# Layer-norm Newton steps on GpSimd, a routing store on ScalarE's queue, one bias tile, and the down products between gate and up

## The reference

```python
def ffn(x):                         # x: (4, 512, 256)
    w = golden_weights(x, Wr, temperature)      # 8 weights for each token
    gate = einsum('btd,edf->betf', x, Wg)       # 8 experts, F = 256
    up   = einsum('btd,edf->betf', x, Wu)
    e_out = einsum('betf,efd->betd', silu(gate) * up, Wd)
    return einsum('bte,betd->btd', w, e_out)

x = x + 0.5 * ffn(layernorm(x))
x = x + attention(layernorm(x))     # causal, 16 heads of 16, biases on q, k, v and the output
x = x + 0.5 * ffn(layernorm(x))
```

## Time and profile before

| | |
|---|---|
| three runs | 883.81, 884.58 (median), 886.05 us |
| the profiled execution, its time | 883.35 us |
| its span, first to last instruction | 881.6 us |
| TensorE busy | 792.5 us (90%) |
| VectorE busy | 508.9 us (58%) |
| GpSimd busy | 383.7 us (44%) |
| ScalarE busy | 344.4 us (39%) |
| mean granted TensorE clock | 0.973 |

### The profile page before, as it was taken

The page is one execution under the profiler, slowest core; times in us unless marked ns, Lnnn a source line. Parts: engine busy times, 40 slices in busy tenths (PEclk is TensorE's granted clock), DMA queues, the critical chain, the costliest instruction groups (busy, mean ns, idle before and its releaser), DMA issues.

```text
span 881.6 us, 13749 instructions
## 1 busy us (share of the span) xinstructions
PE 792.5 (90%) x4856; PEld 617.4 (70%) x4856; DVE 508.9 (58%) x1424; ACT 344.4 (39%) x656; POOL 383.7 (44%) x365
## 2 busy tenths in 40 slices
PE   3397897989988999979999897899999999999997
PEld 3286786857656676667767666677667677888886
DVE  5367677485666753586754466855446743475332
ACT  3134334424355343244533335444325344232321
POOL 3064564236432453242344334245344455446664
PEclk9889899999999999998999999999999999999999
DMA  4534433514412422221252213234222223222331
GB/s 155 168 108 144 120 109 96 140 53 108 106 58 77 121 74 86 60 72 55 84 151 73 73 55 90 73 109 108 94 76 73 74 73 96 72 72 80 125 108 49
DMA packets 60617, 81.93 MB, mean 93 GB/s; under 512 B 8066, under 2 KB 44162, under 8 KB 60548
## 3 DMA queue, kind: packets, MB, share of 16 engines
q1 hardware_dynamic: 58816, 80.90, 30.5%
q10 hardware_dynamic: 1732, 0.15, 0.1%
HBM read 68.17 MB, written 12.71 MB: 92 GB/s over the span
## 4 chain that ended last, share of the span: by engine, by line
PE 66%; DVE 21%; issue 3%; ACT 3%; DMA 3%; SPq 2%; POOL 1%; POOLq 0%; DVEq 0%; ACTq 0%
PE gu L408 10%; PE gu L410 10%; PE gu L409 10%; PE dn L427 5%; PE dn L428 5%; PE dn L429 5%; PE ra L517 4%; PE ra L490 4%; PE ra L505 3%; DVE junk L856 3%; PE ra L385 2%; DVE hid L821 2%; DVE hid L814 2%; PE ra L481 2%; SPq L992 1%
## 5 line engine op out<-in xcount | busy, mean ns | idle before, releaser
L912 POOL TENSOR_TENSOR hid<-hid,wb 128x512 f32<-128x512 f32 x128 | 167.7, 1311 | 299.0 <-DVE hid L821 267.0
L408 PE MATMUL gu<-xt_hi,wgu_hi 128*128 128x512 f32 x512 | 232.4, 454 | 16.6 <-DVE hid L814 16.6
L916 POOL TENSOR_TENSOR ht_lo<-hid,ht_hi 128x512 fp32r<-128x512 f32 x128 | 165.6, 1293 | 159.1 <-ACT ht_hi L619 159.0
L856 DVE CUSTOM_DVE_ANT_0 junk<-ra,mask 128x128 bf16<-128x128 f32 (+3 forms) x256 | 124.0, 488 | 161.0 <-PE ra L490 159.7
L410 PE MATMUL gu<-xt_lo,wgu_hi 128*128 128x512 f32 x512 | 206.1, 403 | 0.0
L409 PE MATMUL gu<-xt_hi,wgu_lo 128*128 128x512 f32 x512 | 204.9, 400 | 0.0
L427 PE MATMUL dn<-wd,ht_hi 128*128 128x256 f32 x512 | 164.8, 322 | 1.3 <-POOL ht_lo L916 1.3
L664 ACT ACTIVATE probs<-ra 128x512 f32<-128x512 f32 x160 | 95.4, 597 | 171.6 <-PE ra L505 170.9
L814 DVE SCALAR_TENSOR_TENSOR hid<-hid,gu 128x512 f32<-128x512 f32 x128 | 87.6, 684 | 122.4 <-ACT hid L612 121.9
L619 ACT ACTIVATE ht_hi<-hid 128x512 fp32r<-128x512 f32 x128 | 80.4, 628 | 187.9 <-POOL hid L912 166.9
L428 PE MATMUL dn<-wd,ht_hi 128*128 128x256 f32 x512 | 145.7, 285 | 0.0
(11 more groups left out here) (126 smaller groups left out, 859.2 us busy)
## 6 DMA issues: line engine op xcount, KB each, us to landing
wd<-wd_parts SPq DMA_DIRECT2D x56, 512.0 KB, 3.5
wb<-wts_rows SPq DMA_DIRECT2D x64, 256.0 KB, 3.9
qk_parts<-parts SPq DMA_DIRECT2D x32, 192.0 KB, 2.1
q_st<-qk_parts SPq DMA_DIRECT2D x96, 64.0 KB, 3.3
k_st<-qk_parts SPq DMA_DIRECT2D x96, 64.0 KB, 2.5
wd_parts<-wd SPq DMA_DIRECT2D x8, 512.0 KB, 5.1
x_res<-in_x SPq DMA_DIRECT2D x4, 512.0 KB, 6.5
stage<-in_Wg SPq DMA_DIRECT2D x8, 256.0 KB, 3.9
```

The source lines that it names most:

```text
L408: mm(b_, w_hi, xt_hi[q % 2][:, c, :], start=c == 0, stop=False)
L856: nc.vector.tensor_tensor_reduce(out=junk[:, USE[it] % NA, 0:w], in0=o[:, 0:w], in1=mask[:, T - w:T], scale=1.0, scalar=-3.0e38, op0=ALU.a ...
L912: nc.gpsimd.tensor_tensor(tb, tb, wb[m % NWB][:, :], ALU.mult).then_inc(hw_done, 1)
L916: nc.gpsimd.tensor_tensor(ht_lo[n % NHT][:, :], hid[n % NHID][:, :], f32(ht_hi[n % NHT][:, :]), ALU.subtract).then_inc(lo_done, 1)
```

## The change

1. **Newton.** Variance and seed stay on VectorE (now `var`), the three Newton steps and the shift go to GpSimd (`newton`, in two halves of 8 and 6 instructions, each waiting for the one before). [...] The first-layer blocks q = 1, 2, 3 are done together, on tiles of 12 instead of 4 columns, during chunks 3.6 to 5.4. There are then 10 sets instead of 12.
2. **Routing store.** For block 0 alone, the store of the weights and the first two loads back are issued by ScalarE right after its copy; ScalarE waits for the store to land before it issues the loads.
3. **Bias.** Since the weights of a token's attention sum to one, v's bias times Wo plus the output bias is one row for all tokens. It is computed once (6 matmuls, item `bias`) and added to the residual by GpSimd (`xb`, 8 additions of 128x512). The 32 matmuls of line 478 go, and so do the small set-up steps for `rows` and `ones`. The load of the output bias is now 128 KB.
4. **Order.** The down products of chunk n - 2 stand between gate and up of chunk n. The times of h, hi and lo move back by a third of a chunk.
5. **Small ones.** The memset of two rows of `k_st` (line 897) becomes a short memset and two small copies by ScalarE's queue. The first weight split (`sg`, 0) moves ahead of the first normalisation. Routing is cut into 8 pieces instead of 5, with the same instructions. The last addition and the output store of a block go in two halves, the first as soon as the first two token tiles are done.

```diff
@@ schedule()
+        put(n + 0.67, ("u", n, 0))
+        put(n + 0.83, ("u", n, 1))
+        put(n + 0.84, ("h", n))
-        put(n + 0.34, ("u", n, 0))
-        put(n + 0.50, ("u", n, 1))
-        put(n + 0.51, ("h", n))
         for i in range(QT):
-            put(n + LAG + 0.66 + 0.08 * i, ("d", n, i))
-        put(n + 0.85, ("hi", n))
-        put(n + 1.35, ("lo", n))
+            put(n + LAG + 0.34 + 0.08 * i, ("d", n, i))
+        put(n + 1.15, ("hi", n))
+        put(n + 1.62, ("lo", n))
...
-        put(2 * e - 3.0 if e else -8.6, ("sg", e))
+        put(2 * e - 3.0 if e else -9.45, ("sg", e))
...
+    for j in range(6):
+        put(3.6 + 0.2 * j, ("stats", 1, j))
+    put(4.9, ("var", 1))
+    put(5.1, ("newton", 1, 0))
+    put(5.4, ("newton", 1, 1))
...
@@ TensorE
-                        pe.wait_ge(rows_done, 2)
...
-                            mm(b_, ones[:, :], rows[:, w - 2, :], start=True, stop=False)
...
@@ ScalarE
+                        if q == 0:
+                            act.wait_ge(*emptied(it))
+                            act.dma_start(wts_dram[q].rearrange("e i t -> (e i) t"), wt[:, :]).then_inc(w_st, 16)
+                    if kind == "wb" and it[1] < NWB:
+                        m = it[1]
+                        act.wait_ge(w_st, 16)
+                        act.dma_start(wb[m][:, :], wts_dram[0, m].rearrange("i t -> (i t)").unsqueeze(0).to_broadcast([P, T])
+                                      ).then_inc(wb_ld[m], 16)
@@ VectorE
+                        for m in range(2):
+                            dve.wait_ge(*((half_done, q + 1) if m == 0 else (down_done, CB * (q + 1))))
...
@@ GpSimd
-                chain(nc.gpsimd.memset(k_st[KROWS:SROWS, :, :, :], -1.0))
+                chain(nc.gpsimd.memset(minus[:, :], -1.0))
...
+                    if kind == "newton":
+                        k, half = it[1:]
+                        tile = slice(STATS_OF[k][0] * QT, STATS_OF[k][1] * QT)
+                        y, v, tmp = rstd[:, tile], var[:, tile], ntmp[:, tile]
+                        pool.wait_ge(var_done, VAR_DONE[k])
+                        for _ in range((2, 1)[half]):
+                            link(nc.gpsimd.tensor_tensor(tmp, y, v, ALU.mult))
+                            link(nc.gpsimd.tensor_tensor(tmp, tmp, y, ALU.mult))
+                            link(nc.gpsimd.tensor_scalar(tmp, tmp, -0.5, 1.5, ALU.mult, ALU.add))
+                            link(nc.gpsimd.tensor_tensor(y, tmp, y, ALU.mult))
+                        if half == 1:
+                            link(nc.gpsimd.tensor_tensor(tmp, mv[:, tile, 0], y, ALU.mult))
+                            nc.gpsimd.tensor_scalar(shift[:, tile], tmp, -1.0, None, ALU.mult).then_inc(st_done, 1)
+                    if kind == "xb":
+                        b, m = it[1:]
+                        xt = x_res[:, b * QT + 2 * m:b * QT + 2 * m + 2, :]
+                        pool.wait_ge(aln_done, 2 * (2 * b + m + 1))
+                        pool.wait_ge(*emptied(("bias",)))
+                        nc.gpsimd.tensor_tensor(xt, xt, bias_all[:, :].unsqueeze(1).to_broadcast([P, 2, D]),
+                                                ALU.add).then_inc(xb_done, 1)
```

More of the change, by code:

```diff
@@ L51 @@
 MASKS = 3
-CONSTS = 9
-ROUTE_PIECES = 5
-RSTD_PIECES = 4
+CONSTS = 7
+ROUTE_PIECES = 8
+NEWTON = 3
+STATS_OF = [(0, 1), (1, BATCH)] + 2 * [(b, b + 1) for b in range(BATCH)]
 def f32(ap):
@@ L104, in schedule @@
         put(2 * (E + k) - 1.0, ("sa", k))
-    for b, t in enumerate((-21, -6.0, -1.0, 3.0)):
+    for b, t in enumerate((-21, -6.0, 0.9, 1.8)):
         put(t, ("ldx", b))
     wt_at = {0: 1.0}
-    put(-9.4, ("small",))
+    put(-9.35, ("small",))
+    put(17.8, ("bias",))
     put(-9.3, ("ln", 0, 0), ("ln", 0, 1))
@@ L113, in schedule @@
     put(1.0, ("wt", 0))
-    for k in range(RSTD_PIECES):
-        put(-9.5, ("rstd", 0, k))
+    put(-9.52, ("stats", 0, 0))
+    put(-9.51, ("stats", 0, 1))
+    put(-9.5, ("var", 0))
+    put(-9.49, ("newton", 0, 0))
+    put(-9.48, ("newton", 0, 1))
+    for j in range(6):
[3 more added lines that the diff above has]
+    put(5.4, ("newton", 1, 1))
     for k in range(ROUTE_PIECES):
-        put(-7.9 + 0.1 * k, ("route", 0, k))
+        put(-7.9 + 0.05 * k, ("route", 0, k))
     for q in range(1, NBLOCK):
         start = CB * (q - 1) + {4: 2.2, 6: 6.8, 7: 8.2}.get(q, 5.0)
-        for k in range(RSTD_PIECES):
-            put(start + 0.25 * k, ("rstd", q, k))
+        if q >= BATCH:
+            s = q - BATCH + 2
+            put(start, ("stats", s, 0))
+            put(start + 0.2, ("stats", s, 1))
+            put(start + 0.4, ("var", s))
+            put(start + 0.6, ("newton", s, 0))
+            put(start + 0.85, ("newton", s, 1))
         put(start + 1.2, ("ln", q, 0))
@@ L138, in schedule @@
         head = meet[0] - (9.8 if b else 7.65)
-        for k in range(RSTD_PIECES):
-            put(head - 1.4 + 0.25 * k, ("arstd", b, k))
+        s = BATCH + 2 + b
+        put(head - 1.4, ("stats", s, 0))
+        put(head - 1.2, ("stats", s, 1))
+        put(head - 1.1, ("var", s))
+        put(head - 0.95, ("newton", s, 0))
+        put(head - 0.7, ("newton", s, 1))
+        for m in range(2):
+            put(head + 3.0 + 2.0 * m, ("xb", b, m))
         put(head - 0.4, ("aln", b, 0))
@@ L224, in build @@
         USE = {it: k for k, it in enumerate(it for it in PE_ORDER if it[0] in RING)}
+        ends = [it[1] for it in POOL_ORDER if it[0] == "newton" and it[2] == 1]
+        STATS_DONE = {("ln", q): ends.index(min(q, 1) if q < BATCH else q - BATCH + 2) + 1 for q in range(NBLOCK)}
+        STATS_DONE |= {("aln", b): ends.index(BATCH + 2 + b) + 1 for b in range(BATCH)}
+        VAR_DONE = {it[1]: k + 1 for k, it in enumerate(it for it in DVE_ORDER if it[0] == "var")}
         XN_BEFORE, latest = {}, {}
@@ L241, in build @@
         bk = sb("bk", [P, KT])
-        rows = sb("rows", [2, 2, D], F32R)
-        ones = sb("ones", [2, P], F32R)
-        sel = sb("sel", [2, 1])
+        bv = sb("bv", [P, KT])
+        bias_all = sb("bias_all", [P, D])
         ident = sb("ident", [P, P])
@@ L286, in build @@
         rec = sb("rec", [P, QT * GH])
+        cn_at = nc.sbuf_base
         cn = sb("cn", [P, QT, D])
@@ L431, in _ @@
                             last.then_inc(down_done, 1)
+                        if k == CB - 1 and i == 1:
+                            last.then_inc(half_done, 1)
                     if kind in ("xt", "x"):
@@ L760, in _ @@
                                                 ALU.subtract).then_inc(r_lo, 1)
-                        dve.wait_ge(r_hi, 2)
-                        dve.wait_ge(consts, 5)
-                        link(nc.vector.scalar_tensor_tensor(out=rows[:, :, :], in0=f32(rows_hi[:, :, :]), scalar=sel[:, 0:1],
-                                                            in1=rows_in[:, :, :], op0=ALU.mult, op1=ALU.add))
+                        dve.wait_ge(consts, 3)
                         link(nc.vector.reciprocal(half_rt[:, :], temp[:, :]))
-                        nc.vector.tensor_scalar(half_rt[:, :], half_rt[:, :], 0.5, None, ALU.mult).then_inc(rows_done, 1)
+                        nc.vector.tensor_scalar(half_rt[:, :], half_rt[:, :], 0.5, None, ALU.mult).then_inc(rt_done, 1)
+                    if kind == "bias":
+                        dve.wait_ge(bv_done, 1)
+                        for c in range(KT):
+                            ins = nc.vector.tensor_scalar(bv_lo[:, c, :], f32(bv_hi[:, c, :]), -1.0, bv[:, c:c + 1], ALU.mult,
+                                                          ALU.add)
+                        ins.then_inc(bv_done, 1)
+                        dve.wait_ge(ra_full, full(it))
+                        nc.vector.tensor_tensor(bias_all[:, :], o[:, 0:D], bias_all[:, :], ALU.add).then_inc(freed, 1)
                     if kind == "sg":
@@ L1027 @@
         "bk": np.ascontiguousarray(raw("attn_bk").reshape(KT, P).T),
-        "rows": np.ascontiguousarray(np.broadcast_to(np.stack([raw("attn_bv"), raw("attn_bo")])[None], (2, 2, D))),
+        "bv": np.ascontiguousarray(raw("attn_bv").reshape(KT, P).T),
+        "bo": row("attn_bo"),
     }
```

152 lines of the change are left out of this document (79 added, 73 removed), and 2 rows, old and new, of the table DELAY.

## The result

The changed kernel takes **860.12 us** (median of four runs, 855.05 to 860.50), the kernel before 884.19 us in the same session (882.88 to 886.05). The ratio is 0.9713, with a 95% interval of 0.9673 to 0.9753: 24 us less, where the prediction had 22. The profiled execution took 860.3 us. A second session gave 856.05 us and a ratio of 0.9651 (0.9623 to 0.9679). The kernel thus moves by a few us from session to session, and what follows compares kernels of one session by their times and kernels of different sessions by their ratios.

The account below looks back on a forecast made before the run. TensorE, busy 792.5 of 881.6 us, was taken as the limit, in the middle together with moments when VectorE is late. Terms: -5.3 - 13 - 9 + 2 + 3 = -22.3 us, giving 862 us, range 846 to 880.

Parts of the forecast that it names:

- The ones matmuls: The 32 matmuls of line 478 cost 0.50 us each on TensorE; removing them gives -13 us, bounds -15.3 and -8.
- The store: Block 0's routing store is issued earlier from ScalarE's queue than from SyncE's: -5.3 us, bounds -7.5 and -3.1.
- the start stood "at nothing": Before the first normalisation: earlier variance -2.3 us, Newton set on GpSimd +1.6, other early work about +0.7; counted as nothing.
- The first sign: At the start, TensorE's wait is near 7 us instead of 12.70, and GpSimd's first product starts near 36 us.
- Newton leaves VectorE: In the middle, two TensorE waits, 2.78 and 3.03 us, go with their low clock: -9 us, bounds 0 and -18.
- its cost on GpSimd: Newton sets of 3.6 us on GpSimd show only where chunks run alone: +2 us, bounds 0 and +10.
- The order: More even use of the `gu` banks gains nothing, since nobody waits for one after 120 us.
- The pile: At chunk 4, statistics of three blocks done together cause a 4.5 us wait: +3 us, bounds -2 and +7.
- The routing pieces: Routing on VectorE, cut into more pieces, only changes places; counted as nothing.
- The ones matmul costs its columns: Rival: removing the line 478 matmuls is worth only 2.8 us, giving 872 us; chance 0.06.
- Slower: GpSimd's sets hold the chain: Rival: GpSimd's Newton sets delay the down products in the middle too, 900 us at 0.6 us an instruction; chance 0.10.
- The gain in the middle is swallowed: Rival: VectorE's row maxima set the pace, turning half of the 13 and all of the 9 us into waits, 878 us; chance 0.12.

Follow-up runs that it names:

- newton_dve: The changed kernel with the ten Newton sets and the shift put back on VectorE: 851.37 us, ratio 0.9636.
- old_order: The changed kernel with each chunk's down products back behind both up products, Newton still on GpSimd: 851.10 us, ratio 0.9615.
- dve_old_order: The changed kernel with Newton back on VectorE and the down products back behind both up products: 860.45 us, ratio 0.9719.
- no_ones: The kernel before without the 32 matmuls of line 478, biases left out: 867.43 us against 883.57, ratio 0.9830.
- pile_undone: The changed kernel with statistics and Newton sets of blocks 1 to 3 one by one, Newton still on GpSimd: 855.34 us, ratio 0.9682.

## Why the prediction was right, and where it was not

The total was right (862 forecast, 860 and 856 measured), and so was the largest term. Two steps were wrong, Newton's and the order's. That the total came out all the same is luck: the gain that Newton's move did not bring was made up by terms that stood too low or at nothing (the ones matmuls, the order, perhaps the routing pieces and the pile).

**The ones matmuls (-13).** Right as to place and price, and perhaps too low as to how much reaches the end: I took 85%, the run's median shows all, -16.1, and its interval allows both. The bias product that replaces them costs more than the 0.7 us counted: TensorE also stands still for 2.11 us ahead of it, before 126.69 us, until VectorE has split the bias (125.59 to 126.59 us).

**The store (-5.3).** Right at the start: undone, it lengthens TensorE's wait by 5.4 us, the two transfers together taking as long from either queue. At the end the median shows -3.5, with intervals that overlap, so 5.3 is not ruled out. What the kernel before and the changed kernel show side by side is 1.0 us less, because the head of the program is longer (the start stood "at nothing"). The first sign held: TensorE waits 7.41 us in place of 12.70. This wait is not the longest of the kernel before, as the prediction has it: TensorE's first instruction comes at 13.00 us, after a wait for the normalised input.

**Newton leaves VectorE (-9) and its cost on GpSimd (+2).** This is the step that failed, and it failed by what surrounds it. In the old order the move is worth 0.9719 to 0.9615, some -9 us: the forecast of -7 in all would have been near. In the new order, which the changed kernel has, nothing of it is seen; by the medians it costs 1.3 or 6.8 us. The piece's price was right (0.28 us from one to the next against 0.26, three of the 140 longer, 0.60 to 1.22 us).

What was wrong is first the -9: it took two waits, 2.78 and 3.03 us, as Newton's alone, and in `newton_dve` they are gone with Newton on VectorE too. The longest wait of the middle, 3.11 us before 392.82, was not priced at all.

Second, the cost. That a set shows only where chunks run alone is what the trace has: of the seven waits for `ht_lo` two stand where attention runs between the chunks, 0.37 us before 135.87 and 0.31 us before 237.60. But the sum counted only block 7's set. Against `newton_dve`, TensorE waits 2.1 us more for `ht_lo` at the start (7.41 and 5.27), 2.6 us more at the pile (4.26 and 1.64), and 1.3 us more for the first normalised input (13.96 and 12.63). With all rows, that is 6.2 us more for `ht_lo`, 2.3 more for the normalised input and 3.5 more of low clock, less 4.4 that VectorE saves at the ring: 7.6 of the 10.5 us between the two spans.

The margin from the end of each chunk's `ht_lo` (L916 before, L980 after) to the first of its down products (L427, L458) fell, over chunks 20 to 95, from a median of 8.7 us (least 5.0) to 3.7 us (least 0.05). Nearly all of that is the order's doing: in `newton_dve` it is 3.8 us (least 1.3), in `old_order`, with GpSimd's sets, 8.1 us (least 5.1). So "about 4 or more remain" held for the median only, and GpSimd's sets used up what the order had left of the least.

**The order (at nothing).** Wrong, and the larger mistake. Alone it gains 9.3 us, with Newton on VectorE in the changed kernel 7, and with Newton on GpSimd it seems to lose some 5 (851.10 against 856.05, with intervals that overlap). I had argued that nobody waits for a `gu` bank after 120 us, and looked no further; where it gains, single waits in the middle are shorter and the clock is higher.

**The pile (+3).** The wait was forecast to a quarter of a microsecond, 4.26 against 4.5. Its worth was not: nothing that can be told in the new order, -3.6 by the medians in the old. What was left out is that two whole sets less run in the middle; that this is the cause is argued, not shown.

**The routing pieces ("only change places").** By the medians they are worth -5.5 in the one surrounding where they were tried, with intervals that overlap a little. That smaller bunches on VectorE empty the ring sooner fits the 3.2 us less of waits for `mx`; the rest of the difference is not explained.

**The sum.** From the kernel before to `dve_old_order`: -16.1 (ones), +2.8 (the bias product and its wait), -3.5 (store), -5.5 (routing), -3.6 (pile) is -25.9, and -25.3 was measured. The terms come from different surroundings, and three of them (store, routing, pile) are smaller than the intervals can tell, so that the sum closes is a sign and no proof. The last two moves together add -0.5 to -6.

**The rivals.** "The ones matmul costs its columns" is ruled out by `no_ones`. "Slower: GpSimd's sets hold the chain" named a mechanism that is there at the start and at the pile, not in the middle, and its point of decision, 0.46 us a piece, was not reached at 0.28. With it the prediction said that the trace shows only VectorE's small instructions stretched; it shows GpSimd's too (last section). "The gain in the middle is swallowed" is half true: 6.4 us of the idle time went where some 12 were forecast, and 78.8 us of waits are left of 83.9.

What stays open: the session-to-session scatter of the changed kernel (0.9713 and 0.9651) is as large as what Newton's place and the order are worth beside it. That the two gains do not add up is clear (added up they would make 0.953, and the pair has 0.9651 at best); whether each is a loss beside the other is not. And the table shows by which waits these kernels differ, in one profile of each, but no run takes the clock's part away by itself. Nor is the clock settled by the waits: after the wait of 3.27 us before 514.07 it was 0.64 and 0.67 in the two stretches shown, and in `pile_undone`, after the same wait (3.29 us, before 515.55), it was 0.83 and 1.00 in the same two.

By the medians two kernels are faster than both of the pair compared here: the changed kernel with Newton on VectorE (0.9636) or with the old order (0.9615), by 0.2 to 1% over the changed kernel; against its second session (0.9651) the intervals overlap.

## What to carry to other kernels

Two edits that relieve the same wait, or that use the same slack, must not be priced one by one: here one was worth 7 us alone, the other 9, and the pair 0.5 to 6; both shorten the same waits of the middle, and one takes the margin in which the other was hidden. Before moving work to an idle engine, look at the least margin of the chain that it joins, in the order that will be run, not at the median or at the busy share. And a matmul's price is the spacing of its neighbours: a tile of two rows cost four times one of 128, and the cure was as simple as more rows.

## What the runs showed of the hardware

A matmul whose operands have 2 rows, in a row of 128-row ones, cost 0.50 us; with 128 rows and the same columns it cost 0.12 us.

GpSimd's instructions on 128x4 tiles last 0.20 us and follow each other, when chained, at 0.28 us; 128x12 ones at 0.29 us. While VectorE runs an instruction that reads two tiles of SBUF they can last longer. The first row is GpSimd's, the second VectorE's, in the first set of the changed kernel:

```profile
9.20 1.22 POOL L957 TENSOR_TENSOR ntmp<-ntmp,rstd 128x4 f32<-128x4 f32 x1
```

```profile
9.14 1.22 DVE L806 TENSOR_TENSOR wgu_lo<-stage,wgu_hi 128x1024 fp32r<-128x1024 f32 x1 [1.50 <-ACT wgu_hi L608]
```

The small one lasts about as long as the large one runs. The kernel before has the same, which the prediction overlooked: a product of GpSimd that usually takes 1.3 us took 2.21 (VectorE's row first):

```profile
49.43 1.22 DVE L770 TENSOR_TENSOR wgu_lo<-stage,wgu_hi 128x1024 fp32r<-128x1024 f32 x1
49.59 2.21 POOL L912 TENSOR_TENSOR hid<-hid,wb 128x512 f32<-128x512 f32 x1 [0.71 <-DVE hid L821]
```

The Trainium skill, "GPSIMD Engine Reference", Key points, says that GpSimd shares its SBUF interfaces with VectorE, with contention where VectorE's instruction has two SBUF inputs. These rows agree: VectorE's has two, and it is GpSimd's that lasts longer.

The same store landed after 2.4 us from ScalarE's queue and 5.9 us from SyncE's, and the same two loads after 7.4 and 3.7 us: what one gained the other lost, and the change of queue was worth the earlier issue alone.
